# A routed expert layer: a threshold search for eight experts at once, turned into two searches for four experts each

## The reference

```python
probs = softmax(xr @ gate_w.T)                 # xr: the turned tokens, [4096, 8]
# a token is assigned to the experts of its largest probabilities until their sum reaches 0.9
R     = where(assigned, probs - rank, -1e9)    # per token and expert
keep  = top 512 tokens of each expert by R     # capacity = 4096 / 8
score = where(assigned & keep, probs, 0)
h     = gelu(xr @ w1[e].T)                     # 512 x 512 per expert, erf form
out   = x + sum over e of score[:, e] * (h @ w2[e].T)
```

## Time and profile before

| | |
|---|---|
| median of 3 runs | 260.74 us (260.37 to 260.89) |
| profiled execution: time, span | 259.92 us, 258.1 us |
| TensorE matmul busy | 239.8 us (93% of the span) |
| VectorE busy | 199.7 us (77%) |
| ScalarE busy | 148.9 us (58%) |
| GpSimd busy | 135.3 us (52%) |
| granted clock of TensorE, mean | 1.000 |
| moved by DMA | 53.76 MB |

### The profile page before, as it was taken

The page is one execution under the profiler, slowest core; times in us unless marked ns, Lnnn a source line. Parts: engine busy times, 40 slices in busy tenths (PEclk is TensorE's granted clock), DMA queues, the critical chain, the costliest instruction groups (busy, mean ns, idle before and its releaser), DMA issues.

```text
span 258.1 us, 3767 instructions
## 1 busy us (share of the span) xinstructions
PE 239.8 (93%) x1310; PEld 180.6 (70%) x1310; DVE 199.7 (77%) x443; ACT 148.9 (58%) x272; POOL 135.3 (52%) x105
## 2 busy tenths in 40 slices
PE   7677887789999999999999999999999999999993
PEld 2234432236998888888888888888888888888782
DVE  5288899999989997978996799679778966971231
ACT  4261048871757658746864776587468747853300
POOL 1000000027871487887578747884975684277732
PEclk9999999999999999999999999999999999999999
DMA  6999998817779497789649946985696385066342
GB/s 240 423 420 407 492 374 289 320 62 204 235 257 449 93 297 174 174 173 286 183 49 242 241 126 90 275 221 102 122 307 185 46 174 111 0 81 85 92 152 81
DMA packets 12818, 53.76 MB, mean 208 GB/s; under 512 B 2768, under 2 KB 3152, under 8 KB 9552
## 3 DMA queue, kind: packets, MB, share of 16 engines
q1 hardware_dynamic: 4544, 35.68, 38.2%
q0 software_dynamic: 8256, 17.85, 33.8%
HBM read 44.74 MB, written 18.22 MB: 244 GB/s over the span
## 4 chain that ended last, share of the span: by engine, by line
PE 79%; DVE 10%; DMA 8%; issue 1%; POOL 1%; SPq 0%; ACT 0%; DVEq 0%
PE bank L886 11%; PE bank L888 11%; PE bank L887 11%; PE bank L901 10%; PE bank L902 10%; PE bank L906 10%; DMA region<-in_xt 6%; PE bank L867 5%; DVE region L728 5%; PE bank L927 2%; PE bank L932 1%; PE bank L928 1%; DMA xg<-in_x,gath 1%; PE bank L960 1%; PE bank L978 1%
## 5 line engine op out<-in xcount | busy, mean ns | idle before, releaser
L320 POOL DMA_INDIRECT out<-ysb,scat x32 | 61.1, 1909 | 44.4 <-ACT ysb L399 24.4
L533 DVE SCALAR_TENSOR_TENSOR w1rot<-w1raw,rot,w1rot 128x512 f32<-128x512 f32 x84 | 63.0, 751 | 4.8 <-ACT w1rot L358 2.6
L886 PE MATMUL bank<-w2h,hh 128*128 128x512 f32 x128 | 51.3, 401 | 0.0
L888 PE MATMUL bank<-w2h,hl 128*128 128x512 f32 x128 | 50.1, 391 | 0.0
L887 PE MATMUL bank<-w2l,hh 128*128 128x512 f32 x128 | 50.0, 391 | 0.0
L304 POOL DMA_INDIRECT xg<-in_x,gath x16 | 17.0, 1060 | 59.8 <-DVE gath L586 55.5
L901 PE MATMUL bank<-xh,w1h 128*128 128x512 f32 x112 | 44.1, 393 | 0.0
L902 PE MATMUL bank<-xh,w1l 128*128 128x512 f32 x112 | 43.6, 390 | 0.0
L564 DVE TENSOR_TENSOR hl<-hf,hh 128x512 fp32r<-128x512 f32 x32 | 21.9, 688 | 26.5 <-ACT hh L390 26.5
L386 ACT ACTIVATE hf<-bank 128x512 f32<-128x512 f32 x32 | 19.1, 598 | 38.5 <-PE bank L906 32.9
L312 POOL DMA_INDIRECT score<-probs_scratch,pidx x32 | 33.6, 1050 | 9.8 <-issue 9.4
(11 more groups left out here) (144 smaller groups left out, 363.2 us busy)
## 6 DMA issues: line engine op xcount, KB each, us to landing
region<-in_xt SPq DMA_DIRECT2D x8, 1024.0 KB, 9.2
w1raw<-in_w SPq DMA_DIRECT2D x8, 1024.0 KB, 12.2
w2raw<-in_w SPq DMA_DIRECT2D x8, 1024.0 KB
out<-in_x SPq DMA_DIRECT2D x1, 6656.0 KB, 33.5
out<-in_x SPq DMA_DIRECT2D x1, 1536.0 KB, 8.4
score<-probs_scratch,pidx POOLq DMA_INDIRECT x32
out<-ysb,scat POOLq DMA_INDIRECT x32, 5.9
probs_scratch<-probs SPq DMA_DIRECT2D x1, 384.0 KB, 20.1
```

Source lines behind the costliest of these rows:

```text
L320: pool.indirect_dma_start(out_d, bass.IndirectOffsetOnAxis(scat[:, e, s:s + 1], 0), ysb[:, s, :], None, compute_op=ALU.add if e < LAST els ...
L533: ins = nc.vector.scalar_tensor_tensor(dst, w1raw[:, e % 2, i, :], rot[:, j, i:i + 1], dst, ALU.mult, ALU.add)
L886: nc.tensor.matmul(dst, ah, bh, start=first, stop=False)
L888: return nc.tensor.matmul(dst, al, bh, start=False, stop=last)
```

## The change

The eight experts become two sets of four. The keys of a set are put on the partitions twice (t, k, e): 16 groups, 2 copies (`KP`), 4 experts. The two copies try different thresholds, so four columns (`KC`) try eight thresholds per round (before: seven columns, seven thresholds). The duplicate of the keys is written by GpSimd (`spread_keys`), that of the last chunk of set 0 by VectorE. Two matmuls add the counts instead of one.

Set 0 (experts 0 to 3) is searched in the front, in each round two columns on VectorE and two on ScalarE, with one fold per round instead of two; the last four folds run later. Set 1 (experts 4 to 7) has all its four columns on ScalarE (`signs(1, r, ...)`); its rounds 0 and 1 lie before the first layer of expert 0, rounds 2 and 3 in expert 0, rounds 4 to 6 in expert 1. Each has a step on VectorE (`step_set`) and two matmuls (`count_keys`). `count_tokens`, `count_before` and `rows_out` have a third part for experts 4 to 7, in expert 2. The slots of expert 4 move back within expert 2. The base of the thresholds is no longer kept beside them but goes into constants ("delta"). `EARLY` falls from 13/16 to 11/16 of the rows. Before the first layer TensorE now waits for one part of w1 at a time.

```diff
-KV, KA = 4, 3
-KT = KV + KA
+SETS, SE = 2, E // 2
+KP = 2
+KC = 4
+KT = KP * KC
-EARLY = 13 * N // 16
+EARLY = 11 * N // 16
@@ GpSimd, ahead of gather_x(0)
+            for c in range(len(CHUNKS) - 1):
+                pool.wait_ge(key_ready, c + 1)
+                spread_keys(0, *CHUNKS[c])
+            pool.wait_ge(key_ready, len(CHUNKS))
+            spread_keys(1, 0, NT)
@@ ScalarE
+            def signs(q, r, cols):
+                act.wait_ge(thr_ready, done(q, r))
+                if q + r >= 2:
+                    act.wait_ge(cnt_mm, done(q, r) - 2)
+                for c in cols:
+                    last = nc.scalar.activation(hits[:, c, :], keys[:, q, :], ACT.Sign, bias=first_thr(q, r)[:, c:c + 1],
+                                                accum_out=cnt[:, r % 2, c:c + 1])
+                if cols[-1] == KC - 1:
+                    last.then_inc(cnt_a, 1)
...
-                for k in range(KV, KT):
...
+                signs(0, r, (2, 3))
...
+            signs(1, 0, (0, 1, 2, 3))
+            rows_out(0, 0, 2)
+            w1_folded(2)
+            w1_high(0, 2)
+            w2_high(0)
+            signs(1, 1, (0, 1, 2, 3))
             w1_folded(3)
             w1_high(0, 3)
-            rows_out(0, 0, 2)
-            w2_high(0)
             nc.scalar.activation(warm[:, :], cfv("ident")[:, 0:1], ACT.Gelu)
             x_high0(0)
             x_high0(1)
+            signs(1, 2, (0, 1, 2, 3))
...
+                if e == 1:
+                    signs(1, 5, (0, 1))
                 hidden(e, 1)
...
+                if e == 1:
+                    signs(1, 5, (2, 3))
                 hidden(e, 2)
                 if e == 0:
+                    signs(1, 3, (0, 1, 2, 3))
                     hidden(0, 3)
@@ VectorE
+            def step_set(q, r):
+                count_passed(q, r)
+                if r + 1 < ROUNDS:
+                    next_thr(q, r)
+                    move_on(q, r)
+                else:
+                    close_edge(q)
...
+            scale_keys(1, keys[:, 1, :])
             w1_low(0, 0, 1)
...
             slot_tables(0)
+            step_set(1, 0)
             slots_after(1)
...
                 h_low(e, 2)
+                if e == 1:
+                    step_set(1, 5)
...
                     rotate_w1(e + 1, 2)
                 if e >= 1:
                     h_low(e, 3)
+                if e == 2:
+                    slot_tables(4)
                 if e >= 1 and more:
                     x_low(e + 1, 0)
@@ TensorE
+            def count_keys(q, r):
+                if q == 0:
+                    pe.wait_ge(cnt_v, r + 1)
+                elif r in (2, 3):
+                    pe.wait_ge(slots_ready, r)
+                elif r == 6:
+                    pe.wait_ge(slots_ready, 4)
+                pe.wait_ge(cnt_a, done(q, r))
+                for k in range(KP):
+                    last = nc.tensor.matmul(set_counts(q, r)[:, k * KC:(k + 1) * KC], chv("chunks")[:, k * P:(k + 1) * P],
+                                            cnt[:, r % 2, :], start=True, stop=True)
+                last.then_inc(cnt_mm, 1)
...
                     layer1_half(3)
+                    count_keys(1, 3)
...
                     layer1(e, 3)
+                    if e == 1:
+                        count_keys(1, 5)
+                    if e == 2:
+                        slot_rows(4)
```

More of the change, by code:

```diff
@@ new lines, in scale_keys, with scale_back, count_passed @@
+            def scale_keys(q, raw):
+                nc.vector.tensor_scalar(keys[:, q, :], raw, top[:, q:q + 1], scale[:, q, 0:1], ALU.subtract,
+                                        ALU.mult).then_inc(thr_ready, 1)
+            def scale_back(q):
+                nc.vector.tensor_scalar(scale[:, q, 1:2], scale[:, q, 0:1], 3.0, -0.5 if q == 0 else 0.5, ALU.add, ALU.mult)
+                nc.vector.tensor_scalar(scale[:, q, 2:3], scale[:, q, 0:1], 3.0, -0.5 * KEY_ULP, ALU.add, ALU.mult)
+            def count_passed(q, r):
+                dve.wait_ge(cnt_mm, done(q, r))
+                then(nc.vector.scalar_tensor_tensor(passed[:, :], set_counts(q, r), 0.0, table("need", q, 0, KT), ALU.add,
+                                                    ALU.is_ge, accum_out=best[:, :]))
@@ new lines, in next_thr, with move_on @@
+            def next_thr(q, r):
+                ahead_of = table("second", q) if r == 0 else nxt[:, :]
+                nc.vector.scalar_tensor_tensor(thr[:, (r + 1) % 2, :], table("step", q, r), best[:, :], ahead_of, ALU.mult,
+                                               ALU.add).then_inc(thr_ready, 1)
+                dve.wait_ge(thr_ready, done(q, r + 1))
+            def move_on(q, r):
+                there = nc.vector.tensor_tensor(nxt[:, :], thr[:, (r + 1) % 2, :], table("delta", q, r), ALU.add)
+                if r + 2 == ROUNDS:
+                    then(there)
+                    nc.vector.tensor_scalar(edge[:, 0:1], nxt[:, 0:1], scale[:, q, 1:2], top[:, q:q + 1], ALU.mult, ALU.add)
@@ L745, in _ @@
-                dve.wait_ge(cnt_mm, r + 1)
-                then(nc.vector.scalar_tensor_tensor(passed[:, :], cbank[now][:, 0:KT], 0.0, cgv("need"), ALU.add,
-                                                    ALU.is_ge, accum_out=best[:, :]))
-                if r + 1 < ROUNDS:
-                    nc.vector.scalar_tensor_tensor(thr[:, new, :], table("step", r), best[:, :], nxt[:, :], ALU.mult,
-                                                   ALU.add).then_inc(thr_ready, 1)
-                    dve.wait_ge(thr_ready, r + 2)
-                else:
-                    nc.vector.scalar_tensor_tensor(edge[:, 1:2], scale[:, 2:3], best[:, :], edge[:, 0:1],
-                                                   ALU.mult, ALU.add).then_inc(base_ready, 1)
+                    close_edge(0)
@@ L1048, in _ @@
             keep_clock(2, nbank)
[L1049 to L1052 removed]
+            spread_edge(0)
+            folds(11, 12)
             def count_before(n, e0, e1):
@@ L1106, in _ @@
                     layer2(e, s)
+                    if e == 1 and s == 2:
+                        count_keys(1, 6)
+                    if e == 1 and s == 3:
+                        spread_edge(1)
 def shape_constants():
@@ L1143, in shape_constants @@
     ch[:, CH["rowbase"][0] + 1] = np.where(p > 0, NT, -NT * (P - 1))
-    ch[:, slice(*CH["chunks"])] = p[:, None] % E == p[None] % E
+    same = member[:, None] == member[None]
+    ch[:, slice(*CH["chunks"])] = np.concatenate([same & (part == i)[:, None] for i in range(KP)], axis=1)
     ch[:, slice(*CH["lower"])] = p[:, None] < p[None]
```

245 lines of the change are left out of this document (155 added, 90 removed).

## The result

| | before | after |
|---|---|---|
| median of 6 runs each, same chip | 260.56 us | 262.45 us |
| range of the runs | 259.58 to 260.89 | 262.06 to 262.73 |
| profiled execution: time, span | 259.92, 258.1 us | 262.53, 260.7 us |
| TensorE matmul busy | 239.8 us (93%) | 238.0 us (91%) |
| VectorE busy | 199.7 us (77%) | 198.1 us (76%) |

The ratio is 1.0077, 95% interval [1.0059, 1.0096]: the change costs 1.9 us. On another chip the changed kernel gave 262.24 us and the one before 260.47, ratio 1.0068 [1.0047, 1.0089].

What follows compares the result with a forecast made beforehand. TensorE was taken as the bound from the first layer on, VectorE's search ahead of it. Start -2.13, matmuls +0.85, waits +0.5, +1.0 and +0.63 gave +0.85 us: 261.6 us on the median, range 259.8 to 262.8.

Steps and rivals of the forecast that it cites:

- my own case: The main case for the whole kernel: a loss of 0.5 to 1.8 us, 261.2 to 262.6, chance 0.45.
- The search: In the front: a round takes 1.87 us instead of 2.44, ScalarE ending last; seven rounds save 4.0 us.
- From `edge` to the first layer: In the front: ScalarE's long order holds the first layer until 59.95, so it starts only 2.13 us earlier, not 3.7.
- The wait in expert 0: Ahead of `count_keys(1, 3)`: TensorE waits 0.5 us for ScalarE's tests, which stand behind its third Gelu.
- The wait in expert 1: In the first layer 2: TensorE waits 1.0 us for `h_low(1, 3)`, queued on VectorE behind `step_set(1, 5)`.
- The wait in expert 2: Ahead of expert 3's last transposes: TensorE waits 0.63 us, as `slot_tables(4)` moves ahead of `x_low(3, 0)`.
- The matmuls put in: In TensorE's full stream through the experts: added counting and edge matmuls, less the moved `slot_rows(4)`, cost 0.85 us.
- Profile to median: On the whole time: the profiled execution lies 0.8 us below the median, so 260.8 becomes 261.6.
- Tokens start layer 1: Rival in the front: token arrival, not ScalarE, sets the first layer's start, 3.7 us earlier; 260.0 us, chance 0.12.
- No waits: Rival in the experts: TensorE meets none of the three waits, a gain of 1.3 us; 259.5 us, chance 0.07.
- The out copy: Rival in expert 1: a slower late copy delays scatters 4 us and stops layer 2; 264 us, chance 0.06.
- Tables: Rival: `Sign` outside the Gelu set needs twelve loads, 271 us; chance 0.04 together with a clock fall to 1.2 GHz (264).

Runs made afterwards that it cites:

- `no_second_search`: The changed kernel without the search for experts 4 to 7 (all tests, steps and counts of set 1 left out): 259.91 us.
- `one_column`: The changed kernel with one ScalarE test instead of four in round 1 of set 1: 261.62 us.
- `count3_late`: The changed kernel with the count of round 3 of set 1 behind the first transposes for expert 1 instead of ahead of them: 261.98 us.
- `count5_early`: The changed kernel with the count of round 5 of set 1 one quarter of layer 1 of expert 1 earlier: 261.13 us.
- `tables4_late`: The changed kernel with `slot_tables(4)` behind `x_low(3, 0)` and `x_low(3, 1)` instead of ahead of them: 262.14 us.
- `mended`: The changed kernel with the moves of `three_moves` and the edits of `scalar_order` together: 259.44 us.
- `scalar_order`: The changed kernel with the Gelu table load ahead of set 1's round 1 tests, `w2_high(0)` behind two x copies, two unused matmuls fewer: 261.87 us.
- `three_moves`: The changed kernel with the moves of `count5_early`, `count3_late` and `tables4_late` together: 260.02 us.

## Why the prediction was right, and where its terms were off

Predicted 261.6 us (259.8 to 262.8) and more likely slower than not; measured 262.45. The mechanism is the one forecast: a front that gets faster, a start of layer 1 that ScalarE holds, and three waits in the experts that cost more than the front gives. All three were at the places named, with the releasers named, and the runs that remove each bring back 0.6 to 0.95. The size is another matter. Against the medians I forecast a loss of 0.86 us and 1.9 was measured, just outside the 0.5 to 1.8 of my own case. That the time lies inside its 261.2 to 262.6 is luck: with three more runs the median of before came down from 260.74 to 260.56. At the full clock the sum is short by 1.2, 0.35 of it in the front and 0.8 in the experts.

- **The search: right in kind, 0.54 too good.** ScalarE ends last and the round is 1.10 + 0.14 + 0.69 = 1.93, where I had 1.10 + 0.05 + 0.72. The mis-sized part is the 0.05, read behind VectorE's sum and used behind ScalarE's; it is 0.14, there and in expert 0 (74.65 to 74.79). The mean from round to round is 1.955, 0.085 over mine, 0.5 over six rounds. The engine need not be the reason. At 57.46 a count starts 0.05 behind ScalarE's sum (57.22 + 0.19 = 57.41), after a wait just as real. `count_keys` has one wait there, for `cnt_a`. In the places with 0.14 it has two, and the one for `cnt_a` is the second and the last to be met. Before, `cnt_v` came last and is waited for first. So the order of the two waits explains the figures too, and swapping them was not tried.
- **From `edge` to the first layer: 11.96 measured, 12.05 walked.** As a sum it holds, and ScalarE had no gap behind its thresholds. But as a cause it was only half of it. I named the tests; `no_second_search` and `one_column` show the moved folds 0.5 to 0.6 behind them. In my prediction "the last four folds run later" had no price at all.
- **The wait in expert 0: 0.5 predicted, 0.48 of idle time measured.** I reckoned from start to start, though, and so it is 0.64: ScalarE's third Gelu waits for the rotation as I had allowed, but by 0.26 and not 0.18, and the signal is 0.14 and not 0.06. The pair of counts there cost 0.24, not 0.06. `count3_late` gave 0.82.
- **The wait in expert 1: 1.0 predicted, 1.04 measured.** `count5_early` gave 0.95.
- **The wait in expert 2: 0.63 predicted, 0.69 measured.** `tables4_late` gave 0.64.
- **The matmuls put in: 0.85 predicted, about 1.0 measured.** My own parts add up to 0.89. The smaller `count_before(1)` gave, with the pair of round 2 in it, 0.21 where I had 0.20; `count_before(2)` took 0.48 of 0.46; `spread_edge(1)` 0.23 of 0.3; the move of `slot_rows(4)` gave 0.10 of 0.09. The pairs of rounds 4 and 6 cost 0.16 each, as estimated; the one of round 3 0.24, where I had 0.06.
- **Not in the sum: about 0.4.** 0.2 is in the first half layer (3.14 us for 2.95): a fourth wait of TensorE, for the low part of x, which I did not foresee. VectorE's copy ends 0.05 ahead of the weight load that uses it, and the four matmuls take 0.58 instead of 0.48, as they do in `mended`, where the profile names that wait. No run takes it away. The other 0.2 is spread over the stream.
- **Profile to median: 0.8 added.** I took it for a fixed distance between the profiled execution and the median. It is the clock: the profile of before was an execution at 1.000, whose group has its median at 259.98, 0.06 above it. The change at full clock gives 262.13. So the sum of +0.85 was 1.2 to 1.3 too low against the 2.0 to 2.15 there, and the 0.8 hid part of that in the time.
- **The rivals.** "Tokens start layer 1" did not come. With ScalarE's order mended the start is 24.59 behind the keys, 2.9 better than before, and what holds it is still the tests, through ScalarE's order and the count ahead of the transposes. In `no_second_search` the transposes begin 0.79 earlier; an estimate from that is a start at 23.8 (22.24, and the 1.56 from transposes to first layer in `scalar_order`), the 3.7 of my rival. "No waits" was wrong for the change, and `three_moves` shows what it would have been: a draw, not a gain of 1.3, because the search gave less and the stream took more than I had. The out copy moved the first scatter by 2.3 us, where I had it staying in place, and cost nothing. Tables did not change between the tests and the Gelus: three loads in all, as before. The clock did not fall by the sparser rounds in this trace (1.00 from 40 to 45 us).

What stays open: why the clock falls in some executions and not in others, and why a count starts 0.14 us behind ScalarE's sum in most places and 0.05 in one.

## What to carry to other kernels

Work moved from the front of a kernel into the stream of the engine that bounds it has three prices: its own matmuls, the broken rhythm at each place, and the order of the engines that feed it. Here the first two took 1.2 us and the third 2.6, and the third was mostly a matter of places in a written order: three moved lines gave back 2.4 us, with no work changed. Before moving an exchange between engines into a full stream, look in the trace for the instruction queued behind it and for its slack; put the count where the partner's answer is needed a block later, not at once. And price what is pushed out of a stage as carefully as what is taken out: the folds were free in the search, and became the second bound of the start.

## What the runs showed of the hardware

- From the end of ScalarE's sum (the accumulator read) to the matmul that waits for it: 0.14 us where TensorE's code waits for another semaphore first (46.40 to 46.54, 74.65 to 74.79), 0.05 where it waits for this one alone (57.41 to 57.46). From VectorE's, waited for first: 0.05. Which of engine and order of waits makes the difference was not tested.
- A pair of fp16 matmuls of 4 columns between float32 ones costs 0.16 us where it stands alone in the stream (rounds 4 and 6), 0.24 behind a wait (74.79 to 75.03), and 0.05 beside transposes (74.44 to 74.49 in `count3_late`).
- TensorE's granted clock can fall to 1.2 GHz for between 3 and 4 us in a front that waits for loads (0.85, 0.50 and 0.80 in the three windows of 2 us from 10 us of after). In the traces of kernels with this front the key scaling comes between 34.30 us (mean clock 0.998) and 35.16 (0.985). Two profiles can be compared only from a point behind it.
